# Bias adds moved behind the query stores, and key-weight lower parts moved behind the copies of transposed x

## Reference

```
x = x + cross_attention(layernorm(x), ctx)      # 16 heads of 64, weights Wq Wk Wv Wo, biases bq bk bv bo
x = x + self_attention(layernorm(x))            # 16 heads of 32
x = x + expert_attention(layernorm(x))          # 16 experts, gated q, k, v, o projections
# cross_attention, the part that the change touches:
q = ln(x) @ Wq + bq;  k = ctx @ Wk + bk;  v = ctx @ Wv + bv
out = softmax(q k^T / 8) v @ Wo + bo
```

## Time and profile before

| what | value |
|---|---|
| median of 3 runs | 1503.95 us (1503.4 to 1504.15) |
| the profiled execution's own time | 1505.97 us |
| its span, first to last instruction | 1504.2 us |
| TensorE busy | 1449.8 us, 96% of the span |
| VectorE, ScalarE, GpSimd busy | 739.4, 502.8, 173.8 us |
| mean granted TensorE clock | 0.978 of full speed |

### The profile page before, as it was taken

The page is one execution under the profiler, slowest core; times in us unless marked ns, Lnnn a source line. Parts: engine busy times, 40 slices in busy tenths (PEclk is TensorE's granted clock), DMA queues, the critical chain, the costliest instruction groups (busy, mean ns, idle before and its releaser), DMA issues. The chain is left out here.

```text
span 1504.2 us, 22239 instructions
## 1 busy us (share of the span) xinstructions
PE 1449.8 (96%) x8564; PEld 1115.5 (74%) x8564; DVE 739.4 (49%) x1644; ACT 502.8 (33%) x1111; POOL 173.8 (12%) x150
## 2 busy tenths in 40 slices
PE   5999999999999999999999999999999599799999
PEld 4667777777777777777777777777777377588777
DVE  5335433463354336434533463354335555577679
ACT  3115421471153136413421471153124424321111
POOL 3211000130020003101000130020000112100012
PEclk9999999999999999999999999999999897899999
DMA  6511000140010003201000140010011130023300
GB/s 210 174 65 43 19 12 11 39 134 1 11 50 12 11 8 105 61 11 32 18 12 12 39 134 1 11 43 5 4 60 57 16 112 1 26 88 100 96 30 29
DMA packets 44359, 71.50 MB, mean 48 GB/s; under 512 B 8048, under 2 KB 16272, under 8 KB 43616
## 3 DMA queue, kind: packets, MB, share of 16 engines
q1 hardware_dynamic: 42608, 65.04, 14.1%
q0 software_dynamic: 1648, 5.04, 1.1%
HBM read 64.82 MB, written 5.24 MB: 47 GB/s over the span
## 5 line engine op out<-in xcount | busy, mean ns | idle before, releaser
L404 PE MATMUL b_ps<-b_ctxT,wk 128*128 128x512 f32 x1536 | 388.0, 401 | 0.0
L382 PE MATMUL b_ps<-wv,b_ctxT 128*128 128x512 f32 x1536 | 373.2, 401 | 12.4 <-DVE b_ctxT L582 12.4
L382 PEld LDWEIGHTS b_ps<-wv,b_ctxT 128*128 128x128 f32 x1536 | 289.4, 190 | 86.6 <-issue 20.9
L404 PEld LDWEIGHTS b_ps<-b_ctxT,wk 128*128 128x128 f32 x1536 | 279.9, 189 | 58.1 <-issue 1.5
L686 DVE TENSOR_SCALAR_CACHE_REDUCE b_prob<-b_ps 128x512 f32<-128x512 f32 x256 | 166.6, 688 | 309.4 <-PE b_ps L420 309.4
L553 ACT COPY b_pT<-b_ps 128x512 f32<-128x512 f32 x128 | 75.1, 587 | 539.0 <-PE b_ps L433 529.4
L595 DVE COPY b_V<-b_ps 128x512 f32<-128x512 f32 x128 | 88.4, 691 | 250.8 <-PE b_ps L382 250.8
L562 ACT ACTIVATE b_prob<-b_prob,b_negm 128x512 f32<-128x512 f32 x256 | 182.9, 719 | 2.2 <-DVE b_negm L692 2.2
L451 PE MATMUL b_ps<-b_pT,b_V 128*64 128x128 f32 x2048 | 145.5, 279 | 0.3 <-ACT b_pT L553 0.3
L451 PEld LDWEIGHTS b_ps<-b_pT,b_V 128*64 128x64 f32 x2048 | 110.3, 136 | 46.4 <-issue 45.9
L433 PE MATMUL b_ps<-ident,b_prob 128*128 128x128 f32 x1024 | 138.0, 278 | 6.5 <-ACT b_prob L562 6.4
(11 more groups left out here) (201 smaller groups left out, 1249.6 us busy)
## 6 DMA issues: line engine op xcount, KB each, us to landing
stage<-in_ctx SPq DMA_DIRECT2D x64, 256.0 KB, 2.9
stage<-in_Wk SPq DMA_DIRECT2D x30, 256.0 KB, 2.6
stage<-in_Wv SPq DMA_DIRECT2D x28, 256.0 KB, 3.2
b_q<-q_s SPq DMA_DIRECT2D x32, 128.0 KB, 3.0
w_rows<-in_self_w SPq DMA_DIRECT2D x4, 1024.0 KB, 5.0
w_tiles<-in_q_proj SPq DMA_DIRECT2D x16, 256.0 KB, 3.9
w_tiles<-in_k_proj SPq DMA_DIRECT2D x16, 256.0 KB, 3.4
w_tiles<-in_v_proj SPq DMA_DIRECT2D x16, 256.0 KB, 3.4
```

What stands on the lines that cost most here:

```text
L382: mm = nc.tensor.matmul(ps[:, bank], ctxT[:, a, k, n * P:(n + 1) * P], wv[:, w, k], start=m == 0, stop=m == len(terms) - 1)
L404: mm = nc.tensor.matmul(ps[:, bank], wk[:, i % 2, w, k], ctxT[:, a, k, s * BANK:(s + 1) * BANK], start=m == 0, stop=m == len(terms) - 1)
```

## The change

Two pieces of work are moved; none is added or taken away.

1. On GpSimd, the four adds of `bo_b` to x move from their place between its second and third context chunk to behind the loop over the eight query stores. They now wait for all four normalised blocks at once. SyncE's list is the same, with its wait for `xbo_done` ahead of the load of `wo`.
2. The hi and lo parts of the first two Wk pieces (`pre_split` on ScalarE, `pre_rest` on VectorE, n = 4 and 5) move into the prologue's "x" item: on ScalarE behind the copies of context chunks 4, 5 and 6, on VectorE behind the four copies into `xnT`.

```
@@ GpSimd
             for n in (1, 3):
                 chunk_rest(0, n)
-            pool.wait_ge(bo_in, 16)
-            for b in range(NB):
-                pool.wait_ge(ln[5], b + 1)
-                nc.gpsimd.tensor_tensor(xs[:, b], xs[:, b], bo_b[:], ALU.add).then_inc(xbo_done, 1)
             for j in range(NP):
...
+            pool.wait_ge(bo_in, 16)
+            pool.wait_ge(ln[5], NB)
+            for b in range(NB):
+                nc.gpsimd.tensor_tensor(xs[:, b], xs[:, b], bo_b[:], ALU.add).then_inc(xbo_done, 1)
@@ ScalarE
             split_hi(("ctx", 0, 3))
-            for n in range(C, len(PRE)):
-                pre_split(n)
             act.wait_ge(bq_in, 16)
             for item in G.first:
-                if item[0] == "v" and item[2] + 4 < NC:
+                if item[0] == "x":
+                    for n in range(C, len(PRE)):
+                        pre_split(n)
+                elif item[0] == "v" and item[2] + 4 < NC:
@@ VectorE
             normalise()
-            for n in range(C, len(PRE)):
-                pre_rest(n)
...
                         nc.vector.tensor_copy(xnT[:, :, b * P:(b + 1) * P], ...).then_inc(xT_done, 1)
+                    for n in range(C, len(PRE)):
+                        pre_rest(n)
```

## The result

The changed kernel takes 1510.07 us, the median of six runs (1504.73 to 1512.03); the kernel before takes 1503.2 us in its six runs (1502.3 to 1504.15). The ratio is 1.0043, with a 95% interval from 1.0026 to 1.0060: slower by 0.43%, some 6.5 us. The profiled execution has a span of 1508.8 us, 4.6 more than before, and its own time is 1510.59 us.

What follows compares the result with a forecast made beforehand. TensorE, busy 1449.8 of 1504.2 us, was taken as the bound. Front gain -5.0, query stall +8.2 and low clock +2.0 made +5.2 on the 1503.95 median: 1509.2 us, range 1504.5 to 1514.

Steps and rivals of the forecast that it cites:

- the mechanism of the late queries: Prologue's end: late adds delay `wo`, first query tiles queue behind it, TensorE waits; a net cost, chance 0.78.
- VectorE at the front: Front of prologue: normalised blocks end at about 20.6, Wk parts leave the path, third block's transposes start 3.5 us earlier.
- TensorE's gap shrinks to 2.2 us ... I take it that the clock stays up.: Transposes of x: gap 2.2 instead of 5.7 us, clock stays full, adding 0.5 and 1.0 us to the gain.
- The adds: GpSimd, behind the last query store: four bias adds take 5.2 us from about 91.7, complete at 96.8.
- The queue: SyncE's loads: `wo` issued at 96.8 takes 7.6 us, landing at 104.4; first queries land behind it at 105.3.
- The stall: First score product, main loop's start: TensorE waits for the first query tile from 97.1 to 105.3, 8.2 us.
- The clock behind it: After the wait for the first query tile: clock low, back some 4.5 us after restart; costs 2.0 us (1.5 to 3.0).
- The sum at the main loop: Main loop: front gain -5.0, query wait +8.2, low clock +2.0, in all +5.2 us.
- From there every step lies some 5 us later.: From the wait for the first query tile onward, every later step lies some 5 us later than before.
- Rival (a): Prologue's end: query tiles do not queue behind `wo`; stall 3.6 us, sum -0.7, 1503.3 us; chance 0.10.
- Rival (b): Front of prologue: the gain does not come, `xnT` copies held by something hidden; +10.2, 1514.2 us; chance 0.08.
- (c): Prologue's end: stall much shorter because adds or wait were misread; say 1499 us; chance 0.04.

Runs made afterwards that it cites:

- adds_only: Kernel before with only the four bias adds moved behind the last query store, Wk parts in their old place; ratio 1.0043.
- q_behind_adds: Changed kernel with the first two query tiles issued ahead of `wo`, still behind the wait for the adds; ratio 0.9985.
- q_free: Changed kernel with the first two query tiles and first four weight pieces issued ahead of the two waits and of `wo`; ratio 0.9974.
- spread: Changed kernel with one bias add behind each of the first four query stores instead of all four behind the last; ratio 0.9973.
- spread_fill: Changed kernel with one bias add behind each of the first four query stores, plus 14 unused TensorE products between second and third transpose blocks; ratio 0.9961.
- fill: Changed kernel with 35 unused TensorE products ahead of the first score product; ratio 1.0029.
- wk_only: Changed kernel with the four bias adds back in their old place, so only the Wk parts are moved; ratio 0.9982.

## Why the prediction was right

The forecast was slower, 1509.2 us in a range from 1504.5 to 1514, by the mechanism of the late queries; measured 1510.07. That the late queries are the cause is shown by three runs: adds_only has the whole loss, q_behind_adds takes 6.9 of the 9.1 us away by the order of two transfers, q_free all of it with the adds left where the change put them. By its steps:

- **VectorE at the front.** Right. The blocks of normalised x are 2.90 us, the two Wk parts have gone from the path, and chunk 4's landing is what comes late next: VectorE waits there for 2.32 us. The prediction let the blocks end at about 20.6; by its own terms (0.46, 1.44, 0.46 and 0.55 from 17.25) it is 20.2, and nothing hung on it, since chunk 4 comes later. Set against its own start (0.9 us earlier), the third block came 3.4 us sooner; 3.5 was forecast.
- **"TensorE's gap shrinks to 2.2 us ... I take it that the clock stays up."** This step failed. The gap was 3.19 us and the clock fell 2.3 us after TensorE had stopped at 22.21, where the earlier trace rows had it after 3.4. The 24 value products took 7.80 us, more than the 7.13 of before, and not 6.14. So the extra 1.5 us of the gain did not come, and the gain at the main loop was 3.6; without the earlier start it is 2.7, below the lower end of 3.5. The length of the gap is only part of it. It differs because the third block starts 13.9 to 14.0 us after the first value product in all five runs with this front and the gap left empty, while the 36 value products ahead of it took from 9.8 us (here, 21.18 less 11.41) to 10.7 (q_free). In q_free and spread the gap had the forecast length, 2.18 and 2.28 us, and the clock fell all the same, at 26.9 and 26.7, 1.3 and 1.0 us after TensorE had restarted; their 24 value products took 7.37 and 7.39. The size forecast for the whole front, 5.0, was reached only with the gap filled: from the first value product to the first key product it is 84.03 us before, 81.34 in the changed kernel and 78.72 in spread_fill, 5.3 less.
- **The adds.** Right: 5.04 us against 5.2, and `wo` within 0.1 us of their end. They begin at 93.02 and not at 91.7 or so, by the 1.4 us that the gain at the front is smaller.
- **The queue.** Right in kind, a bit small in size: queries at 9.0 us after their issue, where 7.6 for `wo` and 0.95 behind it make 7.6 from the queries' issue. `wo` took 8.8, between the 7.6 taken and the 10.9 of the upper end. In part that was made up by SyncE's issue of `wo`, which took 0.34 us and not 0.89.
- **The stall.** 9.1 us against 8.2. From the issue of `wo` to the landing of the tile it is 9.4 us where 8.5 was forecast, and that is the difference.
- **The clock behind it.** 2.5 us against 2.0, and shown to be the clock by fill. It was back 5.6 us after the restart (107.62 to 113.2), not 4.5.
- **The sum at the main loop.** -3.6 + 9.1 + 2.5 = +8.0 against a forecast of +5.2, and it holds to the end of cross attention (1126.55 against 1118.55).
- **"From there every step lies some 5 us later."** Not so to the end of the program. In the profiled execution the rest of the kernel took 3.4 us less than before (382.25 against 385.65), and only 4.6 us are left in the span. The code there is the same. Its windows differ in when the clock is low: in the self-attention stage it is at half from about 1249 to 1267 before, and from about 1260 to 1271 after, with the stage 8 us later. Counted in windows of 1 us from 1188 to 1346, the clock is at half for 58.0 us before and for 51.2 after, and half of that difference is the 3.4 us. In the experiments it is the same: with 57.2 to 58.0 us at half the rest of the kernel takes 385.9 to 386.6 us (wk_only, fill, spread_fill), with 50.5 to 51.2 it takes 382.4 to 383.0 (adds_only, q_free, spread), and q_behind_adds has 41.0 and 381.0. Both groups hold kernels with a loss and kernels with a gain ahead of that point. Why the clock falls sooner or later there is open.
- **Where luck comes in.** The sum at the main loop was 2.8 us too small. The base was 1503.95, where six runs give 1503.2 (0.75 too much), and the medians of the two kernels differ by 6.9 us, 1.1 less than the 8.0 of cross attention. These errors leave 0.9 us between 1509.2 and 1510.07, so that the forecast lies so near has some luck in it. The profiled execution of the kernel before, 1505.97, lies 2.8 us above the median of its six runs, that of the changed kernel 0.5 above its own, which is why the two spans differ by 4.6 us only.

Rival (a), that the tiles do not queue, is refuted by 9.0 us against 2.5 when only the order is changed. The Trainium skill has in "DMA: Bandwidth & Descriptors", section "Queues, rings and completion order", that descriptors are consumed in ring order; the trace agrees with that (9.0 behind `wo`, 2.5 ahead of it). The same page of the Trainium skill, section "Anatomy of one DMA — SWDGE (gpsimd) path", has the fit that gave an estimate of 6.8 us for 2 MB; it is a fit of transfers that GpSimd issues, and `wo`, issued by SyncE, took 8.8.

The order on SyncE's queue may not be all of it. In the kernel before, GpSimd issued two query stores on its own queue at 65.10 and 65.66, while `wo` was in flight (62.84 to 73.7):

```profile
q_s<-b_qhi POOLq DMA_DIRECT2D x1, 256.0 KB, 8.0
q_s<-b_qlo POOLq DMA_DIRECT2D x1, 256.0 KB, 8.8
```

The pair ahead of `wo`, issued at 58.88 and 59.44, took 2.3 and 2.6 us. So a transfer on another queue is slow too beside `wo`; whether a query tile issued there would have come sooner than 9 us was not tried.

Rival (b), no gain at the front, is refuted by wk_only and the third block's start; (c) by the adds' place behind the last query store in the trace and the 9.1 us wait.

## What to carry to other kernels

When an instruction is moved, ask who waits for its semaphore, and then what stands behind that waiter on its own queue: here four adds whose result is first used at 277 us (in the kernel before) held a 2 MB load, and the load held a 128 KB tile that was wanted at once. A transfer that is needed soon goes ahead of a large one that is not, and a wait that guards only the large one is put behind the small one. A stall costs its own length and then the low clock behind it, 1.5 us after 2.2 us of idling and 2.5 after 9.1 here.

## What the runs showed of the hardware

- The granted clock can fall after TensorE has gone on. In q_behind_adds TensorE idled for 2.2 us and restarted at 100.40; the clock went to 1.2 GHz at about 101.2 and came back at about 104.6. In wk_only it idled for 3.1 us, restarted at 27.57, and the clock fell at 28.3; in spread it idled for 2.3 us, restarted at 25.74, and the clock fell at 26.7. The windows of q_behind_adds:

```profile
101.00:102.00 1.00, 1.00 (x6) 0.60 (x3) 0.56 (x1) 0.00 (x0) 0.00 (x0) 0.61 0.69 279
102.00:103.00 1.00, 1.00 (x4) 0.81 (x3) 1.00 (x5) 0.00 (x0) 0.00 (x0) 0.50 0.95 328
```

- From the stop of TensorE to the fall it was between 2.3 us (changed kernel) and 3.9 us (adds_only) for gaps at one and the same place, so one trace of the kernel before (3.4) was no bound for the next. Unused products in the gap kept the clock up both times that they were tried.
- In the kernel before, the first 11 value products in the trace took 557 to 765 ns each, up to 16.8 us, and the later ones 390 to 398, at a granted clock that reads full speed throughout; in the changed kernel they were fast from about 14.6 on. Over the nine executions the 36 products took from 9.8 to 11.0 us by this. Why is open.
- Beside a GpSimd instruction with two inputs in SBUF, a VectorE instruction with two such inputs took between 0.81 and 1.78 us against 0.68 alone, and one on a PSUM source 0.68 as always. The 1.78 stands twice: in the kernel before beside the bias adds (the first Wk part, at 22.02), and in wk_only beside a context chunk's lower part (at 25.04, above). In wk_only GpSimd had begun 0.03 us earlier and took its usual 1.27; in adds_only VectorE began first, at 23.41, and took 0.68, and GpSimd's lower part, from 23.49, took 1.73.
